# A recommendation tower on one core: the work of the last tile and the last layers put in another order and on other engines

## The reference

```python
x = layer_norm(dense_t @ Wd.T, gd, bd)
y = layer_norm(jnp.einsum('bnd,ed->bne', sparse_t, Ws), gs, bs)
y = layer_norm(jnp.einsum('bne,pn->bep', y, Wsi), gsi, bsi)
T = jnp.concatenate([x[:, None, :], jnp.swapaxes(y, 1, 2)], axis=1)
Zflat = jnp.einsum('bnd,bmd->bnm', T, T)[:, TRIL_I, TRIL_J]
z = layer_norm(Zflat @ Wl.T, gl, bl)[:, :384]
h = jnp.concatenate([z, r_dense_t], axis=1)
h = jnp.maximum(h @ W_top1 + b_top1, 0.0)      # 512
h = jnp.maximum(h @ W_top2 + b_top2, 0.0)      # 256
return h @ W_top3
```

## Time and profile before

| | us |
|---|---|
| runs | 572.42, 573.66, 692.02 |
| profiled execution, its own time | 572.97 |
| its span, first to last instruction | 571.2 |
| TensorE busy | 508.8 (89%) |
| VectorE busy | 397.6 (70%) |
| ScalarE busy | 291.6 (51%) |
| Pool busy | 396.1 (69%) |
| mean granted TensorE clock | 0.976 |

### The profile page before, as it was taken

One profiled execution on the slowest core, in us unless ns is written; L12 is line 12 of the kernel. 1 busy time (PEld: TensorE's weight loads), 2 busy tenths in 40 slices (PEclk: granted clock), 3 DMA queues, 4 the chain that ended last, 5 costly groups with the idle time before them and its releaser, 6 DMA issues.

```text
span 571.2 us, 20128 instructions
## 1 busy us (share of the span) xinstructions
PE 508.8 (89%) x7271; PEld 381.6 (67%) x7271; DVE 397.6 (70%) x708; ACT 291.6 (51%) x760; POOL 396.1 (69%) x417
## 2 busy tenths in 40 slices
PE   1887869999999999999999899998989999899975
PEld 1854546767676767777776677676667767678664
DVE  4677985777776877767776768777666777667800
ACT  1434565646464655555564646545455646455433
POOL 5777777777777777777777777777777777774000
PEclk9979799999999999999999999999989999899998
DMA  7711221313132221313131312213131222213020
GB/s 252 263 29 28 67 52 29 93 28 94 27 81 40 69 51 31 91 27 92 30 91 28 91 32 68 51 31 91 28 90 31 72 46 58 64 29 85 5 62 1
DMA packets 32138, 36.06 MB, mean 63 GB/s; under 512 B 11789, under 2 KB 20950, under 8 KB 32038
## 3 DMA queue, kind: packets, MB, share of 16 engines
q0 software_dynamic: 13248, 13.65, 12.5%
q1 hardware_dynamic: 18790, 21.11, 11.2%
HBM read 25.54 MB, written 9.18 MB: 61 GB/s over the span
## 4 chain that ended last, share of the span: by engine, by line
POOL 50%; issue 20%; PE 17%; DVE 5%; DMA 4%; ACT 3%; DVEq 0%; ACTq 0%
POOL rows L603 50%; PE bank_z L738 5%; DMA rows<-in_table,ids_based 3%; PE bank_b L704 2%; PE bank_z L719 2%; PE bank_z L677 1%; PE bank_z L671 1%; PE bank_aw L692 1%; DVE y L422 1%; PE bank_d L782 1%; PE bank_d L769 1%; DVE r_vec L448 1%; DVE scaled L387 1%; PE bank_aw L769 1%; DVE scaled L412 1%
## 5 line engine op out<-in xcount | busy, mean ns | idle before, releaser
L603 POOL DMA_INDIRECT rows<-in_table,ids_based x411 | 394.6, 960 | 128.2 <-issue 123.4
L432 DVE TENSOR_REDUCE y_var<-y_sq 128x32 f32<-128x1024 f32 x63 | 76.9, 1220 | 41.4 <-ACT y_sq L920 41.2
L920 ACT ACTIVATE y_sq<-y 128x512 f32<-128x512 f32 x128 | 80.3, 631 | 34.3 <-DVE y L422 33.8
L719 PEld LDWEIGHTS bank_z<-r_vec 128*32 128x32 f32 x4096 | 48.5, 111 | 58.2 <-issue 55.4
L704 PE MATMUL bank_b<-mixed,gs_row 64*128 64x512 f32 x128 | 75.7, 673 | 10.3 <-ACT mixed L956 8.7
L448 DVE TENSOR_TENSOR r_vec<-y,bank_z 128x512 f32<-128x512 f32 x128 | 82.4, 684 | 2.3
L440 DVE RECIPROCAL bank_z<-y_std 128x32 f32<-128x32 f32 x63 | 22.7, 361 | 78.0 <-ACT y_std L926 78.0
L949 ACT ACTIVATE row_std<-row_var,eps 128x8 f32<-128x8 f32 (+1 forms) x64 | 19.2, 300 | 111.9 <-DVE row_var L396 102.4
L677 PE MATMUL bank_z<-gram,rows_t 128*128 128x128 f32 x416 | 66.3, 300 | 10.7 <-ACT rows_t L941 10.5
L704 PE MATMUL bank_c<-mixed,gs_row 64*128 64x512 f32 x128 | 75.7, 673 | 0.0
L738 PE MATMUL bank_z<-wl,zd 128*128 128x512 f32 x160 | 75.2, 615 | 0.0
(11 more groups left out here) (123 smaller groups left out, 632.1 us busy)
## 6 DMA issues: line engine op xcount, KB each, us to landing
rows<-in_table SPq DMA_DIRECT2D x640, 0.2 KB
zx<-zs SPq DMA_DIRECT2D x15, 560.0 KB
rows<-in_table,ids_based POOLq DMA_INDIRECT x411
dense_t<-in_dense_t SPq DMA_DIRECT2D x1, 2048.0 KB, 8.6
wl<-in_wl SPq DMA_DIRECT2D x1, 1280.0 KB
w<-in_w SPq DMA_DIRECT2D x1, 1280.0 KB
zd<-zx SPq DMA_DIRECT2D x15, 80.0 KB
zd<-zx SPq DMA_DIRECT2D x15, 70.0 KB
```

The costliest lines, as they stand in the source:

```text
L432: v.tensor_reduce(y_var[:, k % BANKS, :], y_sq[:, k % 2, :, :].rearrange("e a (s p) -> e (a s) p", p=PROJ), AX_X, ALU.add).then_inc(y_var_ ...
L603: nc.gpsimd.indirect_dma_start(rows[t % ROWS_KEPT][:, c, D * blk:D * (blk + 1)], None, io["table"], bass.IndirectOffsetOnAxis(ap=ids_all[: ...
L719: mm = pe.matmul(bank_i[PROJ * s:PROJ * (s + 1), n * ITEMS:(n + 1) * ITEMS], own[:, Y0:PAD], own, start=True, stop=True)
L920: nc.scalar.activation(y_sq[:, k % 2, blk, :], y[:, k % 2, blk, :], ACT.Square).then_inc(y_squared, 1)
```

## The change

Only the end of the kernel is touched.

- The dense part of tile 14's first layer (`first_dense_14`) is computed in step 56 into `bank_l`, copied to SBUF by ScalarE in step 57 (`keep_dense_14`), and added by VectorE to the products on z (`add_dense_14`); before, it ran in the end list.
- The orders of TensorE, VectorE and ScalarE behind step 60 are written anew: turning, Gram product, squaring and scaling of rows of quarters 62 and 63 stand earlier, layers of tiles 13 and 14 later.
- The scalings of `y` for quarters 60, 61 and 62 run on Pool behind the last gather (`y_scale_pool`), with the reciprocals in SBUF (`y_r_last`) in place of PSUM; that of 63 stays on VectorE in halves. Copies of `y` and `interact` wait for Pool's semaphore instead.
- Tile 15: `keep_turned_z` runs on VectorE in three parts, each with its own count; the first layer goes in two halves into two banks, the second layer's two output halves into two banks, and the ReLUs follow by halves. `second_layer(14)` stands between `linear(15)` and `turn_z(15)`, `third_layer(14)` behind the first layer of tile 15.

The diff, cut to its core ("..." marks what is left out):

```diff
-        bank_lin = [bank_l] * (TILES - 2) + [bank_t] * 2
-        bank_h1 = [bank_d] * (TILES - 2) + [bank_l, bank_m]
-        bank_h2 = [bank_d] * (TILES - 1) + [bank_b]
-        bank_o = [bank_d] * (TILES - 1) + [bank_c]
+        bank_lin = [bank_l] * (TILES - 1) + [bank_t]
+        bank_h1 = [[bank_d] * 4] * (TILES - 2) + [[bank_b] * 4, [bank_a, bank_a, bank_w, bank_w]]
+        bank_h2 = [[bank_d] * 2] * (TILES - 2) + [[bank_c] * 2, [bank_b, bank_d]]
+        bank_o = [bank_d] * (TILES - 2) + [bank_l, bank_c]
...
-                    dve.wait_ge(r_ready, k - 1)
+                    if k - 2 < TAIL:
+                        dve.wait_ge(r_ready, k - 1)
+                    else:
+                        dve.wait_ge(r_ready_pool, k - 2 - TAIL + 1)
...
+            def y_reciprocal_kept(k):
+                dve.wait_ge(y_std_done, k + 1)
+                v.reciprocal(y_r_last[:, k % BANKS, :], y_std[:, k % BANKS, :]).then_inc(y_r_done, 1)
+
             def y_reciprocal_block(k, blk):
                 dve.wait_ge(y_std_done, k + blk + 1)
-                dve.wait_ge(zs_kept, k)
                 part = slice(blk * SPB, (blk + 1) * SPB)
-                v.reciprocal(y_r[:, part], y_std[:, k % BANKS, part]).then_inc(y_r_done, 1)
+                v.reciprocal(y_r_last[:, k % BANKS, part], y_std[:, k % BANKS, part]).then_inc(y_r_done, 1)
+
+            def y_scale_block(k, blk):
+                dve.wait_ge(y_r_done, k + blk + 1)
+                dve.wait_ge(z_done, k - 3)
+                quad = (2 * (k % BANKS) + blk) * (SPB // QUAD)
+                ins = v.tensor_tensor(
+                    r_vec[:, quad:quad + SPB // QUAD, :, Y0:PAD],
+                    y[:, k % 2, blk, :].rearrange("e (g s p) -> e g s p", g=SPB // QUAD, p=PROJ),
+                    y_r_last[:, k % BANKS, blk * SPB:(blk + 1) * SPB].rearrange("e (g s o) -> e g s o", s=QUAD, o=1)
+                    .broadcast_to([P, SPB // QUAD, QUAD, PROJ]), ALU.mult)
+                if blk:
+                    ins.then_inc(r_ready, 1)
+
+            def add_dense_14():
+                dve.wait_ge(h1_done, TILES - 1)
+                dve.wait_ge(dense_14_kept, 1)
+                v.tensor_tensor(dense_14[:], bank_b[:].rearrange("p (k n) -> p k n", n=TILE), dense_14[:], ALU.add)\
+                    .then_inc(dense_14_added, 1)
+
+            def keep_turned_z_last():
+                dve.wait_ge(z_turned, TILES)
+                dve.wait_ge(h1_done, TILES - 1)
+                for c in range(3):
+                    v.tensor_scalar(z_t[:, c, :], bank_t[:, c * P:(c + 1) * P], col["gl"][:, c:c + 1],
+                                    col["bl"][:, c:c + 1], ALU.mult, ALU.add).then_inc(z_kept_last, 1)
...
-            end = QUARTERS - 1
-            y_mean_square_block(end, 0)
-            y_mean_square_block(end, 1)
+            y_mean_square(TAIL)
+            square_form(TAIL + 2)
+            row_mean_square(TAIL + 2)
+            y_reciprocal_kept(TAIL)
+            keep_y(TAIL + 1, 0)
+            row_reciprocal(TAIL + 2)
+            scale_rows(TAIL + 2)
+            keep_y(TAIL + 1, 1)
+            y_mean_square(TAIL + 1)
+            square_form(TAIL + 3)
+            row_mean_square(TAIL + 3)
+            y_reciprocal_kept(TAIL + 1)
+            row_reciprocal(TAIL + 3)
+            scale_rows(TAIL + 3)
+            keep_y(TAIL + 2, 0)
+            keep_y(TAIL + 2, 1)
+            y_mean_square(TAIL + 2)
+            y_reciprocal_kept(TAIL + 2)
+            keep_y(TAIL + 3, 0)
+            keep_y(TAIL + 3, 1)
+            y_mean_square_block(TAIL + 3, 0)
+            y_mean_square_block(TAIL + 3, 1)
             for blk in range(2):
-                y_reciprocal_block(end, blk)
-                dve.wait_ge(y_r_done, end + blk + 1)
-                y_scale(end, blk)
+                y_reciprocal_block(TAIL + 3, blk)
+                y_scale_block(TAIL + 3, blk)
             linear_reciprocal(TILES - 2)
+            add_dense_14()
             linear_reciprocal(TILES - 1)
...
+            def y_scale_pool(k):
+                pool.wait_ge(y_r_done, k + 1)
+                pool.wait_ge(z_done, k - 3)
+                for blk in range(2):
+                    quad = (2 * (k % BANKS) + blk) * (SPB // QUAD)
+                    ins = nc.gpsimd.tensor_tensor(
+                        r_vec[:, quad:quad + SPB // QUAD, :, Y0:PAD],
+                        y[:, k % 2, blk, :].rearrange("e (g s p) -> e g s p", g=SPB // QUAD, p=PROJ),
+                        y_r_last[:, k % BANKS, blk * SPB:(blk + 1) * SPB].rearrange("e (g s o) -> e g s o", s=QUAD, o=1)
+                        .broadcast_to([P, SPB // QUAD, QUAD, PROJ]), ALU.mult)
+                ins.then_inc(r_ready_pool, 1)
+
             for k in range(QUARTERS):
                 gather(k)
+
+            for k in range(TAIL, QUARTERS - 1):
+                y_scale_pool(k)
...
+                if k < TAIL:
+                    pe.wait_ge(r_ready, k + 1)
+                elif k < QUARTERS - 1:
+                    pe.wait_ge(r_ready_pool, k - TAIL + 1)
+                else:
+                    pe.wait_ge(r_ready, TAIL + 1)
...
+            def first_dense_14():
+                t = TILES - 2
+                pe.wait_ge(z_kept, t - 1)
+                for k in range(4):
+                    for i in range(2):
+                        mm = pe.matmul(bank_l[:, k * TILE:(k + 1) * TILE], w1[:, 3 + i, k * P:(k + 1) * P],
+                                       dense_t[:, i, t * TILE:(t + 1) * TILE], start=(k + i == 0), stop=(i == 1),
+                                       skip_group_check=True)
+                mm.then_inc(dense_14_done, 1)
...
+            def first_layer_last():
+                t = TILES - 1
+                for half in range(2):
+                    for c in range(3):
+                        if half == 0:
+                            pe.wait_ge(z_kept_last, c + 1)
+                        for k in (2 * half, 2 * half + 1):
+                            n = k % 2 * TILE
+                            mm = pe.matmul(bank_h1[t][k][:, n:n + TILE], w1[:, c, k * P:(k + 1) * P], z_t[:, c, :],
+                                           start=False, stop=(c == 2), skip_group_check=True)
+                    mm.then_inc(h1_done, 1)
...
+            def second_layer_last():
+                t = TILES - 1
+                pe.wait_ge(dense_14_added, 1)
+                pe.wait_ge(out_kept, t - 1)
+                for k in range(2):
+                    for c in range(4):
+                        if k == 0:
+                            pe.wait_ge(h1_kept, 4 * t + c + 1)
+                        mm = pe.matmul(bank_h2[t][k][:, 0:TILE], w2[:, c, k * P:(k + 1) * P], h1[:, c, :],
+                                       start=(c == 0), stop=(c == 3))
+                    mm.then_inc(h2_done, 1)
...
-                first_layer(last - 2, range(4))
-                first_dense(last - 1)
-
+                first_layer(last - 2, range(0, 2))
                 turn(w + 2)
                 mix(w + 1)
                 gram_product(w + 2)
                 project(w + 1)
+                first_layer(last - 2, range(2, 4))
+                mix(w + 2)
+                turn(w + 3)
+                gram_product(w + 3)
                 interact(w)
+                project(w + 2)
+                linear(last - 1, range(0, 1))
+                mix(w + 3)
+                interact(w + 1)
+                project(w + 3)
+                linear(last - 1, range(1, 3))
+                interact(w + 2)
+                linear(last - 1, range(3, STEPS))
+                interact(w + 3)
                 second_layer(last - 2)
-
-                turn(w + 3)
-                mix(w + 2)
-                gram_product(w + 3)
+                turn_z(last - 1)
+                first_dense(last)
                 third_layer(last - 2)
-                project(w + 2)
-                interact(w + 1)
-                linear(last - 1, range(0, 1))
-
-                mix(w + 3)
-                linear(last - 1, range(1, 2))
-                project(w + 3)
-                linear(last - 1, range(2, STEPS))
-                interact(w + 2)
-                first_dense(last)
-                interact(w + 3)
-
-                turn_z(last - 1)
                 first_layer(last - 1, range(4))
+                linear(last, range(STEPS))
                 second_layer(last - 1)
+                turn_z(last)
+                first_layer_last()
                 third_layer(last - 1)
-                linear(last, range(STEPS))
-                turn_z(last)
-                first_layer(last, range(4))
-                second_layer(last)
+                second_layer_last()
                 third_layer(last)
...
                 upper(w)
+                if w == TAIL - BANKS:
+                    first_dense_14()
...
+                    if t < TILES - 2:
+                        h = bank_h1[t][k][:, k * TILE:(k + 1) * TILE]
+                    elif t == TILES - 2:
```

(92 more changed lines are left out.)

22 lines of the change are left out of this document (10 added, 12 removed).

## The result

The changed kernel took 569.84 us (median of 11 runs, 567.74 to 570.94), the kernel before 572.73 beside it. The ratio is 0.9932, interval 0.9913 to 0.995: 3.9 us faster, 2.9 to 5.0. (The ratio is taken over all runs but one; the two medians by themselves differ by 2.9.) The profiled execution's span is 568.0 us, against 571.2. (The one left out is a run of the kernel before of 692.02 us, over 20% above all others.) The forecast was 566.6, that is 7.05 us of gain, in a range of 564 to 572: the range and the direction held, and about half of the size came (3.9 by the ratio, 2.9 by the medians).

The account below looks back on a forecast made before the run. Pool's 411 gathers bound it until 522.33 us, then TensorE's order and a chain of small steps. Gains of 3.25 before interact(63) and 3.8 behind it, 7.05 in all, gave 566.6 us, range 564 to 572.

Parts of the forecast that it names:

- Step 56: Dense part moved into TensorE's 2.29 us wait there: costs nothing, clock should stay up, turn(61) at most 1.0 us earlier.
- The landing of 62: Gathered rows of quarter 62 land 3.9 us after last issue at 516.08: 520.0, bounds 518.5 and 520.5.
- turn(62) to interact(63): Chain of small steps over engines from 520.0 to 540.0, putting interact(63) 3.25 us earlier than 543.25.
- 5.3, to 525.4: First chain piece, turn(62) to mix(62): old 6.3 for quarter 63, less VectorE's y scalings, plus a reciprocal.
- rival 3: Clock falls in the new 1.8 to 2.3 us wait ahead of turn(62): 1.9 us more, 568.5; chance 0.12.
- to scaled rows of 63 4.4: Second chain piece: mix(62) 1.1, turn(63) directly behind it, rows of 63 scaled by 530.9.
- rival 1: Pool and VectorE block each other where rows of 62 and 63 are scaled: 1.6 to 4.2 us; chance 0.20.
- the part that the forecast kept for itself: Time between 564.5 and 568.2 us, the forecast itself without rivals; chance 0.45.
- Pool's price: Pool's scaling of y taken at 1.3 us per instruction, two per quarter; each us beyond costs 4 in the end.
- interact(63) to the end: Last stretch, from interact(63) at 540.0 to span end at 564.15; 3.8 us of the gain lies behind interact(63).
- The slower side: Rival 4: Pool's scalings eat the gain from 3.1 us each on, 579 at 4 us; chance 0.05.

Follow-up runs that it names:

- the held write: Changed kernel plus 16 filling products, reciprocals of rows 62 and 63 in PSUM, zs write of tile 14 held until rows 62 turned; fastest: 565.63 us, 0.9863.
- the two pairs of kernels that differ by it: Reciprocals of rows 62 and 63 in PSUM against SBUF: changed kernel 0.9912 against 0.9932; with 16 filling products 0.988 against 0.9897.
- Pool at twice its price: Fastest kernel (filling, PSUM, held write) with each Pool scaling done once more into an unread tile: 0.9922 against 0.9863, 3.4 us slower.

## Why the prediction was right or wrong

**Step 56: right.** The dense part starts at 485.81 and turn(58) waits 0.16; the clock stays up behind it; turn(61) starts at 511.78, 0.3 earlier (at most 1.0 was said), and the added work alone costs nothing.

**The landing of 62: right.** 520.26 for 520.0, 3.8 us behind the last issue for 3.9, and the held write shows that the write issued beside the gather is the cause.

**turn(62) to interact(63): wrong as made, 23.1 us for 20.0.** The failing step is the first piece of the chain, "5.3, to 525.4": turn(62) to mix(62) took 8.2 us (520.26 to 528.47). It was costed from the old stretch of quarter 63, whose rows are all at the full clock, while the sum itself put a wait of 1.8 to 2.3 us in front, as long as the one ahead of 488.08. That was rival 3, with a chance of 0.12 and 1.9 us; it measured 2.0 in the times. The 12% were too few: the one row with such a wait had such a fall behind it, and "the wait stands behind a busy stretch" was as true of that row (in the kernel before TensorE was busy 1.79 to 2.00 of every two us from 480 to 486). The second piece, "to scaled rows of 63 4.4", and the first once more missed what was rival 1, at 0.20 and 1.6 to 4.2 us: 0.58 and 0.65 us of longer scaling, 1.1 and 1.0 us in the two pairs of kernels that differ by it. The sign named for it, VectorE's scaling held until a Pool instruction ends, is what the traces show. Its price came in below the 1.6 us named for one such wait, for VectorE only waits out what is left of the instruction. Both rivals came true together; the forecast had set their times apart, and 2.0 + 1.0 over the forecast's 566.6 would be 569.6. With both removed, interact(63) came at 539.70. So the order and the other pieces of the chain were right, and its two rivals were the miss. That the time still lies in the range is owed to the range, which was drawn wide enough for the rivals; the part that the forecast kept for itself, 564.5 to 568.2, does not hold 569.84.

The Trainium skill, "SBUF — State Buffer", section "Who interferes with whom", has the rule that rival 1 quoted, and the runs agree with it: one operand moved to PSUM ended the delay, and six scalings with both operands in SBUF ended 0.40 to 0.41 us behind the end of the Pool instruction that they met. What the wait costs is the rest of that instruction, here 0.3 to 0.65 us of longer scaling and never the full 1.05.

**Pool's price: on the safe side.** 2.05 us for two, 1.03 each, where 1.3 was taken between 0.68 and 2.6. By the 2.6 cycles per element of the Trainium skill, "GPSIMD Engine Reference", section 3.1, the estimate was 1.1 to 1.2. With 0.27 less each the chain had 0.5 in hand, and the trace has it: from the end of the reciprocal of 62 to interact(62) it is 2.3 us (538.40 to 540.68) where 2.75 were laid out. What Pool's help brings is 1.3 us by the times (uncertain by 1.9) once nothing else stands in the way, and nothing measurable in the change as it was.

**interact(63) to the end: right, 24.6 us for 24.15.** linear(15) starts 8.9 behind interact(63)'s start where 8.55 were laid out. The last layer takes 2.94 at a clock of 1.00. second_layer(14) covers the wait ahead of turn_z(15), and the kernel before with filling at the end shows that such a cover is worth 1.6 us or more by itself. Turned z by parts on VectorE: 0.50 us of wait, as laid out.

**The slower side** was right to be small: in the fastest kernel, Pool at twice its price still left 4.5 us to the kernel before.

## What to carry to other kernels

A stage freed of its work gets a wait instead, and the products behind that wait may run at half the clock, as they did here behind 2.54 us: look for the longest idle stretch that a new order of TensorE makes, and put independent products there, idle ones if there are none. When elementwise work goes to Pool, see where VectorE's instructions with two SBUF operands fall beside it, and move one small operand to PSUM (1.0 us here, for two such places). And where two rivals in a forecast don't exclude each other, add them.

## What was not expected of the hardware

Adding 1.95 us of products that nothing reads made this kernel faster twice: by 2.0 us ahead of turn(62), and by 2.6 us ahead of turn_z(15) in the kernel before. The granted clock fell behind a wait of 2.54 us, and also behind 1.98 and 1.67 us ahead of mix(62) with 1.65 and 1.30 shortly before; and the same wait of 1.63 us ahead of tile 14's first layer was followed by 24 products in 2.94 us in one execution and in 4.49 in another. A write of 560 KB issued 0.2 to 0.3 us behind the last gather of a quarter went with rows 3.8 to 4.3 us behind that gather; without it they were there within 2.9.
